# Experts' gathered rows turned by DMA transposes of their 16-bit halves in place of TensorE transposes

## The chip, the cores and the metric

The kernel runs on one core of a Trainium2 chip. The metric is the device time of one execution in microseconds; a single launch does everything, and the host only lays the inputs out.

## What is computed

The reference is a gated feed-forward layer with adapters (LoRA), followed by a mixture of eight experts, each token going to its best two. The second part is the one that the change touches:

```python
x = x + ffn(cond(x, ...), W_gate, b_gate, W_e, b_e)     # x: 2048 tokens of 1024

def ffn(y, W_gate, b_gate, W_e, b_e):                   # y: 2048 x 1024, W_e: 8 x 1024 x 1024
    logits = y @ W_gate + b_gate
    _, top_idx = jax.lax.top_k(logits, 2)
    y_all = relu(einsum('bsd,edh->bseh', y, W_e) + b_e)
    return take_along_axis(y_all, top_idx[..., None], axis=2).mean(axis=2)
```

All of it is float32. TensorE gets each float32 operand as a rounded high part and a low part (what rounding left), and each product is three matmuls: high by high, high by low, low by high.

## The kernel before, in words

Two groups of 1024 tokens go through the gated layer and leave y in DRAM (`y_scratch`). Then a table of rows is built: the 4096 pairs of token and expert are sorted by expert and padded to blocks of 128 rows, each block for one expert. There are 41 block numbers at most (`NB`); how many are used is known only at run time, and blocks from 32 on stand under a branch (`when`). In the profiled run 37 are used, numbers 0 to 36.

Five engines work on the blocks, each through its own list in order:

- **GpSimd (POOL)**, for b = 1, 2, ...: `y_lo(b+1)`, the low part of block b+1 (L837); `gather_y(b+3)`, which fetches 128 rows of y into `ybuf`, a ring of three buffers (L829); `add_bias(b)` (L847); `scatter(b)`, which adds the finished rows into the output by DMA (L855).
- **TensorE (PE)**: `one(b)` waits for both parts of block b (`s_tc`, `s_tlo`) and for the expert's weights (`s_el`), does 24 of its 48 matmuls, then `turn(b+1)`, eight 128 x 128 transposes of the next block's rows into PSUM (L2013), then the other 24. The last matmul raises `s_blk`. The rows must be turned because TensorE contracts over partitions, and a gathered row lies along one partition.
- **ScalarE (ACT)**, for b = 2, 3, ...: `blk_hi(b)` copies the turned block from PSUM to `ytp` (L1446) and, rounded, to `ring` (L1447); `blk_out(b-1)` waits for the end of block b-1's matmuls, copies their sums out of PSUM (L1457, raising `s_zc`), waits for the bias and applies relu (L1459).
- **VectorE (DVE)** rounds the next expert's weights (L1672) and takes their low parts (L1673).
- **SyncE (SP)** loads weights in eight pieces of 512 KB for each expert (L416, three buffers) and each expert's bias (L563).

`ytp` is one buffer: `blk_hi(b)` waits for `s_tlo`, so that POOL is done with block b-1 there, and for `s_blk`, so that `ring`'s half is free.

## Time and profile before

| | us |
|---|---|
| median of 3 runs | 1865.73 (1862.27 to 1865.85) |
| the profiled execution | 1862.27 |
| its span, first to last instruction | 1860.4 |
| PE busy in the span | 1817.3 (98%) |
| POOL busy | 1077.1 (58%) |
| ACT busy | 742.2 (40%) |
| mean granted TensorE clock, share of full | 0.991 |

The span is what the profile covers; 1.9 us of the execution lie outside it. Times in the views are counted from the span's start. Busy time of PE overstates its work, since its matmuls overlap: one is shown as 0.39 us, and the next starts 0.23 us after it. The blocks of experts fill the stretch from about 1400 us to the end.

### The profile page before, as it was taken

The numbers are of one execution on the slowest core, as the hardware profiler recorded it, in microseconds if no ns is written. First come the engines' busy times: TensorE is split into PE (matmuls) and PEld (weight loads), VectorE is DVE, ScalarE is ACT, GpSimd is POOL, SyncE is SP. The second block draws the span as 40 slices with busy tenths as digits, with TensorE's granted clock in tenths as the row PEclk, the third lists the DMA queues.
The fourth block names the chain that finished last, engine by engine and source line by source line (L and its number), as shares of the span: only waits on it lengthen the run. The fifth ranks groups of instructions, "written<-read, shape, count | busy, mean of one in ns | idle before, by whom it ended". The sixth has DMA issues, their size and how long they took to land. (4 is left out here: it accounts for less than half of the span.)

```text
span 1860.4 us, 24949 instructions
## 1 busy us (share of the span) xinstructions
PE 1817.3 (98%) x8583; PEld 1511.6 (81%) x8583; DVE 1252.9 (67%) x1500; ACT 742.2 (40%) x1054; POOL 1077.1 (58%) x643
## 2 busy tenths in 40 slices
PE   7899999999999999999999999999999999999997
PEld 6788888888888888888888887888877888888885
DVE  8878787885567797888888886477878543234400
ACT  5544444444543335444434444443322333333332
POOL 2678888873444454456656544444425666666664
PEclk9999999999999999999999999999998999999998
DMA  5556655645577655555665645676634775577543
GB/s 209 171 201 220 227 203 204 237 157 164 191 247 245 221 181 176 180 177 176 205 217 184 213 162 188 217 251 233 206 132 154 222 192 143 141 193 193 149 101 47
DMA packets 128395, 350.32 MB, mean 188 GB/s; under 512 B 15232, under 2 KB 17152, under 8 KB 128000
## 3 DMA queue, kind: packets, MB, share of 16 engines
q1 hardware_dynamic: 110320, 286.94, 45.3%
q0 software_dynamic: 17952, 61.75, 13.8%
q8 instruction: 77, 1.26, 0.3%
q14 instruction: 46, 0.38, 0.1%
HBM read 267.49 MB, written 90.05 MB: 192 GB/s over the span
## 5 line engine op out<-in xcount | busy, mean ns | idle before, releaser
L1680 PE MATMUL PS<-R,ring 128*128 128x512 f32 (+1 forms) x1800 | 709.0, 394 | 21.4 <-DVE R L939 9.3
L1681 PE MATMUL PS<-R,ring 128*128 128x512 f32 (+1 forms) x1800 | 703.7, 391 | 0.0
L1682 PE MATMUL PS<-R,ring 128*128 128x512 f32 (+1 forms) x1800 | 703.2, 391 | 0.0
L1680 PEld LDWEIGHTS PS<-R,ring 128*128 128x128 f32 x1800 | 339.9, 189 | 92.3 <-issue 14.9
L1682 PEld LDWEIGHTS PS<-R,ring 128*128 128x128 f32 x1800 | 339.2, 188 | 72.0
L1681 PEld LDWEIGHTS PS<-R,ring 128*128 128x128 f32 x1800 | 340.2, 189 | 66.0
L769 POOL TENSOR_TENSOR ring<-raw,ring 128x1024 fp32r<-128x1024 f32 x78 | 193.1, 2475 | 269.1 <-ACT ring L895 269.0
L1680 PE MATMUL PS<-ring,R 128*128 128x512 f32 x592 | 231.6, 391 | 1.7 <-DVE FT L1236 1.7
L1681 PE MATMUL PS<-ring,R 128*128 128x512 f32 x592 | 230.8, 390 | 0.0
L1682 PE MATMUL PS<-ring,R 128*128 128x512 f32 x592 | 230.4, 389 | 0.0
L748 POOL DMA_INDIRECT brw<-in_bgu,idx_b x88 | 95.3, 1083 | 227.8 <-DVE R L1060 188.9
L908 DVE TENSOR_TENSOR R<-FT,R 128x1024 fp32r<-128x1024 f32 x70 | 154.9, 2216 | 88.6 <-ACT R L904 88.3
L889 DVE TENSOR_TENSOR ring<-FT,ring 128x512 fp32r<-128x512 f32 x168 | 167.2, 1005 | 57.9 <-ACT ring L885 56.1
L1672 DVE CAST R<-raw 128x1024 fp32r<-128x1024 f32 x56 | 69.6, 1243 | 194.2 <-PE PS L1682 174.0
L885 ACT ACTIVATE ring<-FT 128x512 fp32r<-128x512 f32 x168 | 105.8, 631 | 214.6 <-PE PS L1682 122.0
L895 ACT ACTIVATE ring<-raw 128x1024 fp32r<-128x1024 f32 x78 | 82.7, 1060 | 245.6 <-PE PS L1682 164.8
L889 DVE TENSOR_TENSOR ring<-raw,ring 128x512 fp32r<-128x512 f32 x130 | 163.0, 1261 | 16.1 <-ACT ring L885 15.6
L885 ACT ACTIVATE ring<-raw 128x512 fp32r<-128x512 f32 x130 | 81.6, 630 | 193.6 <-PE PS L1682 147.8
L1142 DVE TENSOR_TENSOR FT<-FT,PS 128x512 f32<-128x512 f32 x168 | 110.6, 679 | 33.8 <-PE PS L1722 33.6
L1680 PEld LDWEIGHTS PS<-ring,R 128*128 128x128 f32 x592 | 111.1, 188 | 25.5 <-DVE FT L1236 2.5
L1682 PEld LDWEIGHTS PS<-ring,R 128*128 128x128 f32 x592 | 111.1, 188 | 23.6
L1681 PEld LDWEIGHTS PS<-ring,R 128*128 128x128 f32 x592 | 111.2, 188 | 21.6
(191 smaller groups left out, 2345.1 us busy)
## 6 DMA issues: line engine op xcount, KB each, us to landing
raw<-in_wp SPq DMA_DIRECT2D x124, 512.0 KB
act_scratch<-FT SPq DMA_DIRECT2D x140, 256.0 KB, 5.0
FT<-act_scratch SPq DMA_DIRECT2D x70, 512.0 KB, 4.3
raw<-in_we SPq DMA_DIRECT2D x64, 512.0 KB
ytp<-in_wgb SPq DMA_DIRECT2D x96, 256.0 KB
raw<-wt_scratch SPq DMA_DIRECT2D x40, 512.0 KB
out<-in_xn SPq DMA_DIRECT2D x17, 512.0 KB, 5.4
y_scratch<-FT SPq DMA_DIRECT2D x7, 1024.0 KB, 6.2
```

Of the source, the lines that this page charges most:

```text
L748: e.indirect_dma_start(out=brw[0:96, j * 512:(j + 1) * 512], out_offset=None, in_=bgu.rearrange("(r a) n -> r (a n)", a=2), in_offset=ioa( ...
L769: e.tensor_tensor(slot2(n, 1), pair(raw_t(i)), slot2(n, 0), ALU.subtract).then_inc(s_lp, 1)
L885: e.activation(slot(op(g, n), 0), w_src(g, n), ACT.Copy).then_inc(s_hi, 1)
L889: e.tensor_tensor(slot(op(g, n), 1), w_src(g, n), slot(op(g, n), 0), ALU.subtract).then_inc(s_lo, 1)
L895: e.activation(slot2(n, 0), pair(raw_t(i)), ACT.Copy).then_inc(s_hi, 2)
L908: e.tensor_tensor(a_ring(j, 1), raw_a(j), a_ring(j, 0), ALU.subtract).then_inc(s_al, 1)
L1142: e.tensor_tensor(c_tile(q, k), tile(E_T + [0, 2, 0, 1][k]), PS[:, bk + [1, 2, 3, 0][k], :], ALU.add).then_inc(s_c, 1)
L1672: link(e.tensor_copy(s_w_t(ex, k, 0), raw_t(i)))
L1680: e.matmul(out_, hi, whi, start=start, stop=False, skip_group_check=True)
L1681: e.matmul(out_, hi, wlo, start=False, stop=False, skip_group_check=True)
L1682: return e.matmul(out_, lo, whi, start=False, stop=stop, skip_group_check=True)
```

## The change

From block 4 on (`TB = 4`), TensorE no longer turns the gathered rows. ScalarE splits each gathered block into the upper and the lower 16 bits of its float32 values (`upper_lower`, two copies into `brw`, which is free by then), starts one DMA transpose of the 128 x 2048 values of 16 bits from its own queue (`across`, into tiles 15 and 16 of `FT`), and later weaves both halves back into float32 values in `ytp` (`blk_hi16`, two copies) before the rounded copy to `ring`. Blocks 0 to 3 keep the old way. `blk_out` is cut in two, `blk_z` (sums out of PSUM) and `blk_out` (relu), and `across` stands between them. `gather_y` waits for `upper_lower` instead of the TensorE transposes before it writes a buffer again.

```diff
         def gather_y(e, b):
-            if b >= 5:
+            if b in (5, 6):
                 e.wait_ge(s_tp, b - 2)
+            if b >= 7:
+                e.wait_ge(s_de, b - 6)
...
+        rows16 = brw[:, :].bitcast(U16)
+        cols16 = tile(SET_E, 2).bitcast(U16).rearrange("p (c r) -> p c r", r=128)
...
+        def halves(ap):
+            return ap.bitcast(U16).rearrange("p (n h) -> p h n", h=2)
+
+        def upper_lower(e, b):
+            e.wait_ge(s_gd[b % 3], 16 * ((b - 2) // 3 + 1))
+            h = halves(ybuf[:, b % 3, :])
+            e.activation(rows16[:, 0:1024], h[:, 1, :], ACT.Copy)
+            e.activation(rows16[:, 1024:2048], h[:, 0, :], ACT.Copy).then_inc(s_de, 1)
+
+        def across(e, b):
+            e.wait_ge(s_de, b - TB + 1)
+            if b > TB:
+                e.wait_ge(s_rc, b - TB)
+            e.dma_start_transpose(out=cols16, in_=rows16).then_inc(s_dt, 16)
+
+        def blk_hi16(e, b):
+            e.wait_ge(s_dt, 16 * (b - TB + 1))
+            e.wait_ge(s_tlo, b)
+            h = halves(ytp[:, :])
+            e.activation(h[:, 1, :], cols16[:, 0:8, :].rearrange("p k r -> p (k r)"), ACT.Copy)
+            e.activation(h[:, 0, :], cols16[:, 8:16, :].rearrange("p k r -> p (k r)"), ACT.Copy).then_inc(s_rc, 1)
+            e.wait_ge(s_blk, b)
+            e.wait_ge(s_rc, b - TB + 1)
+            e.activation(ring_t(b % 2, 0), ytp[:, :], ACT.Copy).then_inc(s_tc, 1)
...
             for b in range(2, NB):
-                when(e, used, b, blk_hi, e, b)
-                if b:
-                    when(e, used, b - 1, blk_out, e, b - 1)
+                when(e, used, b, blk_hi if b < TB else blk_hi16, e, b)
+                if b + 1 >= TB:
+                    when(e, used, b + 1, upper_lower, e, b + 1)
+                when(e, used, b - 1, blk_z, e, b - 1)
+                if b + 1 >= TB:
+                    when(e, used, b + 1, across, e, b + 1)
+                when(e, used, b - 1, blk_out, e, b - 1)
...
                 products(range(mid))
-                if b < 31:
+                if b + 1 < TB:
                     turn(b + 1)
...
             for b in range(2, NB):
-                if b >= 31:
-                    when(e, used, b + 1, turn, b + 1)
                 when(e, used, b, one, b)
```

ScalarE's list in the blocks of experts, before (two turns of the loop; FT here is the staging buffer of the results, PS is PSUM):

```order
780 L1446 ACTIVATE ytp<-PS 128x1024 [waits s_tlo,s_blk,s_tp]
781 L1447 ACTIVATE ring<-PS 128x1024
782 L1457 ACTIVATE FT<-PS 128x1024 [waits s_sc,s_blk]
783 L1459 ACTIVATE FT<-FT 128x1024 [waits s_ba]
784 L1446 ACTIVATE ytp<-PS 128x1024 [waits s_tlo,s_blk,s_tp]
785 L1447 ACTIVATE ring<-PS 128x1024
```

The same place in the changed kernel, one turn of the loop (its line numbers are its own; brw is the buffer of halves, and FT in rows 967 and 970 is `cols16` and `ybuf`):

```order
967 L1478 ACTIVATE ytp<-FT 128x1024 [waits s_tlo,s_dt]
968 L1479 ACTIVATE ytp<-FT 128x1024
969 L1482 ACTIVATE ring<-ytp 128x1024 [waits s_rc,s_blk]
970 L1464 ACTIVATE brw<-FT 128x1024 [waits s_gd2]
971 L1465 ACTIVATE brw<-FT 128x1024
972 L1491 ACTIVATE FT<-PS 128x1024 [waits s_sc,s_blk]
973 L1472 DMA_TRANSPOSE FT<-brw 128x16x128 [waits s_rc,s_de]
974 L1496 ACTIVATE FT<-FT 128x1024 [waits s_ba]
```

Four ScalarE instructions for each block have become seven and a DMA issue, and what the first of them waits for is no longer PE's `s_tp` but the DMA's `s_dt`.

TensorE's list in the middle of block 3, before (ident is the identity matrix, FT is `ybuf`):

```order
6237 L1681 MATMUL PS<-R,ring 128x512
6238 L1682 MATMUL PS<-R,ring 128x512
6239 L2013 MATMUL PS<-ident,FT 128x128 [waits s_tc,s_gd1]
6240 L2013 MATMUL PS<-ident,FT 128x128 x7
6241 L1680 ISA
6242 L1680 MATMUL PS<-R,ring 128x512
```

and in the changed kernel:

```order
6237 L1724 MATMUL PS<-R,ring 128x512
6238 L1725 MATMUL PS<-R,ring 128x512
6239 L1723 ISA
6240 L1723 MATMUL PS<-R,ring 128x512
6241 L1724 ISA
```

The eight transposes are gone there and in every later block, and nothing has taken their place on TensorE.

## Rows read from the trace of the kernel before

**Rows 1.** The page's chain that ended last: shares of the span by engine, by line.

```profile
PE 45%; DVE 1%; issue 1%; DMA 1%; ACT 0%; POOL 0%; POOLq 0%; SPq 0%; ACTq 0%; DVEq 0%
```

**Rows 2.** Busy time by 40 us stretch, granted clock (PEclk), DMA share, GB/s.

```profile
1560.00:1600.00 40.00, 40.00 (x190) 33.35 (x189) 21.95 (x16) 13.26 (x14) 26.92 (x14) 1.00 0.79 211
1600.00:1640.00 40.00, 40.00 (x191) 33.34 (x190) 13.87 (x10) 13.89 (x14) 25.97 (x14) 1.00 0.57 149
```

**Rows 3.** The copy of sums out of PSUM: duration min/median/max in ns, first and last start.

```profile
L1457 ACT ACTIVATE FT<-PS x37: 1024/1029/1030, 1415.8 to 1846.9; 128x1024 f32<-128x1024 f32 x37
```

**Rows 4.** ScalarE in time: start, us, line, operation [idle before <-releaser].

```profile
1470.21 1.03 ACT L1457 ACTIVATE FT<-PS 128x1024 f32<-128x1024 f32 x1 [3.51 <-PE PS L1682]
...
1600.05 1.03 ACT L1457 ACTIVATE FT<-PS 128x1024 f32<-128x1024 f32 x1 [3.54 <-PE PS L1682]
1603.71 1.06 ACT L1459 ACTIVATE FT<-FT 128x1024 f32<-128x1024 f32 x1 [2.62 <-POOL FT L847]
1606.37 1.03 ACT L1446 ACTIVATE ytp<-PS 128x1024 f32<-128x1024 f32 x1 [1.60 <-PE PS L2013]
1607.29 1.02 ACT L1447 ACTIVATE ring<-PS 128x1024 fp32r<-128x1024 f32 x1
1611.83 1.03 ACT L1457 ACTIVATE FT<-PS 128x1024 f32<-128x1024 f32 x1 [3.51 <-PE PS L1682]
...
1835.98 1.03 ACT L1457 ACTIVATE FT<-PS 128x1024 f32<-128x1024 f32 x1 [5.26 <-PE PS L1682]
...
1846.86 1.02 ACT L1457 ACTIVATE FT<-PS 128x1024 f32<-128x1024 f32 x1 [6.17 <-DMA out<-FT,sidx]
```

**Rows 5.** TensorE around one block's transposes, in time.

```profile
1616.61 0.39 PE L1681 MATMUL PS<-R,ring 128*128 x1
1616.84 0.40 PE L1682 MATMUL PS<-R,ring 128*128 x1
1617.07 1.04 PE L2013 MATMUL PS<-ident,FT 128*128 128x128 f32 x8
1617.87 0.47 PE L1680 MATMUL PS<-R,ring 128*128 x1
1618.18 0.39 PE L1681 MATMUL PS<-R,ring 128*128 x1
```

**Rows 6.** GpSimd in time, one block.

```profile
1601.28 2.39 POOL L847 TENSOR_TENSOR FT<-FT 128x1024 f32<-128x1024 f32 x1 [1.15 <-ACT FT L1457]
1605.05 1.59 POOL L855 DMA_INDIRECT out<-FT,sidx  x1 [1.37 <-ACT FT L1459]
1608.40 2.39 POOL L837 TENSOR_TENSOR ring<-ytp,ring 128x1024 fp32r<-128x1024 f32 x1 [1.76 <-ACT ring L1447]
1610.94 0.99 POOL L829 DMA_INDIRECT FT<-y_scratch,gidx  x1 [0.16 <-issue]
```

**Rows 7.** DMAs of the whole run: out<-in, count, KB each, median us from issue to landing.

```profile
FT<-in_be SPq DMA_DIRECT2D x8, 512.0 KB, 4.2
X<-in_xp SPq DMA_DIRECT2D x2, 512.0 KB, 11.6
FT<-y_scratch,gidx POOLq DMA_INDIRECT x36, 8.1
```

**Rows 8.** DMA from 1470 to 1846 us: packets, MB, share of 16 engines; then issues.

```profile
q0 software_dynamic: 8993, 32.78, 42.1%
q1 hardware_dynamic: 6912, 25.17, 19.2%
...
raw<-in_we SPq DMA_DIRECT2D x42, 512.0 KB
FT<-in_be SPq DMA_DIRECT2D x5, 512.0 KB, 4.1
out<-FT,sidx POOLq DMA_INDIRECT x32
FT<-y_scratch,gidx POOLq DMA_INDIRECT x30
```

**Rows 9.** SyncE's queue in time: issue of one expert's eight pieces of weights.

```profile
1510.20 20.74 SPq L416 DMA_DIRECT2D raw<-in_we  x8
```

**Rows 10.** TensorE's idle times early in the run, and the granted clock around them.

```profile
34.44 0.50 PE L1680 MATMUL PS<-R,ring 128*128 128x512 f32 x1 [1.88 <-DVE ring L889]
...
49.71 0.50 PE L1680 MATMUL PS<-R,ring 128*128 128x512 f32 x1 [3.82 <-DVE ring L889]
...
33.00:37.00 4.00, 2.56 (x11) 2.14 (x12) 3.88 (x7) 2.38 (x5) 2.46 (x3) 1.00 0.28 69
50.00:53.00 3.00, 3.00 (x9) 2.35 (x9) 2.94 (x6) 2.59 (x5) 0.00 (x0) 0.54 0.92 283
```

More of the change, by code:

```diff
@@ L10 @@
 U32 = mybir.dt.uint32
+U16 = mybir.dt.uint16
 ALU = mybir.AluOpType
@@ L23 @@
 NB = 41
+TB = 4
 RW = 3
@@ L273, in build @@
         s_blk, s_zr, s_sc = sem("s_blk"), sem("s_zr"), sem("s_sc")
+        s_de, s_dt, s_rc = sem("s_de"), sem("s_dt"), sem("s_rc")
         y_d = nc.dram_tensor("y_scratch", (T, H), F32).ap()
@@ L1447, in blk_hi, with blk_z @@
             e.activation(ring_t(b % 2, 0), tp, ACT.Copy).then_inc(s_tc, 1)
-        def blk_out(e, b):
+        def halves(ap):
[19 more added lines that the diff above has]
+            e.activation(ring_t(b % 2, 0), ytp[:, :], ACT.Copy).then_inc(s_tc, 1)
+        def blk_z(e, b):
             e.wait_ge(s_blk, b + 2)
@@ L1455, in blk_out @@
             z = PS[:, 4 + 2 * (b % 2):6 + 2 * (b % 2), :]
+            e.activation(sbuf2[:, 2 * (b % 2):2 * (b % 2) + 2, :], z, ACT.Copy).then_inc(s_zc, 1)
+        def blk_out(e, b):
             y = sbuf2[:, 2 * (b % 2):2 * (b % 2) + 2, :]
-            e.activation(y, z, ACT.Copy).then_inc(s_zc, 1)
             e.wait_ge(s_ba, b + 2)
@@ L1497, in _ @@
             blk_hi(e, 1)
+            blk_z(e, 0)
             blk_out(e, 0)
@@ L1500, in _ @@
             for b in range(2, NB):
-                when(e, used, b, blk_hi, e, b)
-                if b:
-                    when(e, used, b - 1, blk_out, e, b - 1)
+                when(e, used, b, blk_hi if b < TB else blk_hi16, e, b)
[5 more added lines that the diff above has]
+                when(e, used, b - 1, blk_out, e, b - 1)
+            when(e, used, NB - 1, blk_z, e, NB - 1)
             when(e, used, NB - 1, blk_out, e, NB - 1)
```

## The prediction

> **What bounds the kernel now.** I read the chain of waits first. It is TensorE almost alone, and every other engine has 1% or less [rows 1], so only what shortens or stalls TensorE moves the time. In the blocks of experts TensorE shows no gap at full clock (40.00 us busy of 40.00, PEclk 1.00), while ScalarE works 13 to 14 us and GpSimd 26 to 27 of each 40 [rows 2]. The change reaches only this stage.
>
> The beat of the stage stands in ScalarE's copies out of PSUM, each released by the last matmul of a block: 37 of them [rows 3], from 1600.05 to the next at 1611.83, so 11.78 us for a block; over 32 blocks, (1846.86 - 1470.21) / 32 = 11.77 [rows 4]. What a block takes without transposes also stands in the trace. The last block turns no successor, and it took 1846.86 - 1835.98 = 10.88 us [rows 4]. TensorE's own rows agree: between two matmuls there are 0.23 us, but 1.03 us (1616.84 to 1617.87) across the eight transposes and 0.31 after them [rows 5], so 0.80 + 0.08 = 0.88 us for the turn. I take 11.77 - 10.88 = 0.89 us.
>
> **What is removed.** The turns of blocks 4 to 36 go, 33 of them, which is 33 x 0.89 = 29.4 us if nothing else comes late. Nothing of that is hidden now, since TensorE has no gap.
>
> **What is added, and where it lies.** ScalarE has for each block two copies for the halves, two for the weaving where one copy to ytp stood, and the issue of a DMA. Its nearest row is the relu, SBUF to SBUF, 1.06 us for 1024 columns, where the next copy follows 0.92 us after a copy's start [rows 4]. Copies of 16-bit values with a stride are in no row. I cost them like the float32 copies: half that would be the most a narrower type could give, twice that the most a stride could take. So ScalarE goes from 4.1 to about 7.2 us of a block of 10.9. As busy time that is free; the order of the waits is what costs.
>
> Follow one block. Let 0 be the end of block b-1's matmuls, as ScalarE sees it. Copying the sums starts then. The transpose of block b+1 is queued behind that copy, so it is issued at about 1.0 (0.1 if the queue doesn't wait for the copy). It lands L later. Then come the two weaving copies (0.95 + 1.06), the wait for their own semaphore (0.05, my estimate) and the rounded copy (1.06), together 3.1 us; then GpSimd's low part, 0.09 us later and 2.39 long [rows 4, 6]; then TensorE may begin block b+1, with about 0.1 us for the semaphore. That is 1.0 + L + 3.1 + 0.1 + 2.4 + 0.1 = L + 6.7, and TensorE wants it at 10.9. As block b+1 then runs some 11.1 us with its first weight load and its last matmul's tail, two blocks take at least 17.8 + L. **First loop: one block takes (17.8 + L) / 2.** Behind the weaving on ScalarE stand the halves of block b+2 (two copies, 2.0), and only then the next copy of sums and the next transpose. **Second loop: one block takes L + 3.1 + 2.0 + 1.0 = L + 6.1.** The block takes the largest of 10.88 and these two. The point at which it is as long as before is L = 5.7 (second loop; 5.7 to 5.8 by the first). The bias and relu stay beside it: 1.03 + 2.39 + 1.06 us after the sums, so done at about 4.8, before the transpose has landed. GpSimd's gather is now issued after a later low part, about when block b ends, and has two blocks of time before its rows are wanted. Neither is on the path.
>
> **What L is** is the whole question, and the trace has no DMA transpose. Its nearest rows move the same 512 KB. From below: the bias loads, on a queue of the same kind and in this very stage, land after 4.2 us [rows 7]. From above: loads of x with others in front of them take 11.6 us, and the gathers of this stage, which start on GpSimd, 8.1 [rows 7]. What the transpose meets in the DMA engines can be read too. In 376 us the gathers and scatters hold 42.1% for 62 transfers, 2.6 us of all 16 engines each, and the loads 19.2% for 47, 1.5 us each [rows 8]. The gather is issued at about the end of a block, as the transpose is, and its data would run beside it. I take half of that overlap: L = 4.2 + 1.3 = 5.5. Where weights are being loaded, a piece of 1.5 us stands in the way as well: L = 7.0. One expert's loads are issued over 20.7 us [rows 9], and six experts have theirs in this stretch (five bias loads in it, one just before), so 6 x 20.7 / 11.8 = 10.5 of the 33 blocks.
>
> The sum: 22.5 blocks with L = 5.5 take 11.65 us, a gain of 0.12 each, -2.7 us. 10.5 blocks with L = 7.0 take 13.1 us (second loop), +1.33 each, +14.0 us. Together +11 us on 1862.3 us of the profiled execution, 1873.6. The median is 3.5 us above that execution, so the forecast for a median is 1877.
>
> **Rule against row.** The row nearest to a plain transfer gives L = 4.2. The Trainium skill says in "Advanced Engine Details and Errata", section "X-Bar Transpose (TRN2)", that such transposes are as fast as regular DMAs, about 90% of a plain copy; by this rule L would stay near that row, and the result is rival B. The Trainium skill also says, in "VectorE: DVE Perf Modes", section "The three transpose paths", that a 128 x 128 transpose of 16-bit values takes 1309 ns by DMA and 390 ns on TensorE. This transpose has 16 such tiles, so if they went one after another at that figure, it would be an estimate of 21 us, which speaks against the change and is rival D. No run here shows either.
>
> **The rivals.**
>
> *A, the forecast:* L between 5 and 7, a gain in quiet blocks and a larger loss where weights are loaded. For it: DMA engines are 0.57 to 0.79 busy before the transpose adds its share [rows 2]. Own range 1862 to 1905. Chance 0.30.
>
> *B, hidden:* L stays at 4.2 or below. The first loop gives 11.0, so -0.77 x 33 = -25 us, and at L under 3.9 the full 29.4: 1836 to 1841. For it: the bias loads' 4.2 us were measured in the same stage. Against: those were issued with no gather at the same moment. Chance 0.22.
>
> *E, issue ahead:* the DMA leaves 0.1 us after the block's end, beside the copy of sums. Both loops lose 0.9 us. L = 5.5 gives 11.2 (-0.57 x 22.5 = -13 us), L = 7.0 gives 12.2 (+0.43 x 10.5 = +4.5), together -8: 1857. Chance 0.20.
>
> *C, as slow as a gather:* L = 8.1 in every block. Second loop 14.2, +2.43 x 33 = +80 us: 1946. TensorE then idles 3.3 us in each block. The clock stayed at 1.00, which is 2.4 GHz, after an idle time of 1.88 us, and fell to about half, 1.2 GHz, after one of 3.82 [rows 10]; if it fell here, each block could lose 1.6 us more (eight matmuls of 0.43 instead of 0.23 us). It decides from L = 5.8 on. Against: the gather's 8.1 us hold GpSimd's own making of descriptors. Chance 0.18.
>
> *D, tiles in a row:* the transpose passes its 16 column groups slowly, L = 11.6 or more. Second loop 17.7, +5.9 x 33 = +196 us: 2060 and up. Chance 0.10.
>
> That the change doesn't do what it says I can rule out: the list of TensorE has no transpose after block 2's. In blocks 32 to 36 every step stands under its own branch, ten more for ScalarE in a turn; before, these blocks kept the beat of 11.8 us, but ScalarE had slack then. I allow 0 to 3 us in all.
>
> **How the numbers follow.** The likeliest case is A. A measurement of this kernel can tell about 0.2%, 3.7 us. Faster (under 1862): B 0.22, most of E 0.13, a little of A 0.02, so 0.37. Within: the rest of E 0.06 and 0.06 of A, 0.12. Slower: the rest of A, C and D, 0.51. The range takes in B whole, E, A and C without its clock term: 1837 to 1950, which leaves out D and the worst of C, 0.15 or so, and the hair below B.
>
> **What would show it.** The transpose's time to landing, of which the copies out of PSUM give the beat: with L = 4.2 a beat of 11.0, with 5.5 of 11.65, with 7 of 13.1. ScalarE's weaving copy should wait for the DMA in each block. If TensorE's wait in front of a block's first matmul is for GpSimd's low part and about as long as the beat less 10.9, the loops are right; if it is for weights, the DMA engines are the limit, which I have not costed. Blocks under way of weight loads should be longer than others; if all are alike, my splitting of L is wrong. The forecast falls if the transposes need twice a plain transfer's time, or if 16-bit copies on ScalarE take 2 us.

## The result and the profile after

The changed kernel takes 1954.55 us, the median of 4 runs (1944.23 to 1979.04), against 1865.79 (1862.27 to 1870.13, 4 runs) for the kernel before on the same chip: a ratio of 1.0456, 95% interval 1.0407 to 1.0505. Ratios, here and below, leave out runs over 1.5% above the fastest of their kernel (here 1979.04), while medians are of all runs, so the loss is 89 us by the medians and 85 by the ratio. The forecast was 1877 with a range to 1950; the sign came out as the likelier one, the size is past the end of the range. The profiled execution took 1944.23 us, span 1942.4, which is 82.0 us more than the 1860.4 of before.

The page: busy time, and the chain that ended last, which answers to [rows 1].

```profile
PE 1818.2 (94%) x8319; PEld 1501.4 (77%) x8319; DVE 1247.3 (64%) x1500; ACT 858.5 (44%) x1153; POOL 1078.1 (56%) x643
...
PE 37%; DMA 7%; issue 3%; ACT 3%; DVE 1%; POOL 0%; POOLq 0%; ACTq 0%; SPq 0%; DVEq 0%
```

TensorE had 98% of the span before and 94% now, and 7% of the chain is a DMA. The list of waits says which one (1480 to 1920 us; engine and line, who released it, us in total, times, longest):

```profile
POOL ring L844 <- ACT ring L1482: 125.8, 31, 15.1
...
PE PS L1723 <- issue: 77.0, 20, 14.6
ACT ytp L1478 <- DMA FT<-brw: 71.0, 24, 13.8
DVE R L1715 <- DMA raw<-in_we: 70.5, 21, 11.3
```

Read it from the last but one line upwards: the weave (L1478) waits for the transpose, the low part on GpSimd (L844) waits for ScalarE, and a block's first matmul (L1723) waits, 20 times, for the low part. ("Issue" names no engine here; the rows below show that GpSimd ends 0.2 us before.) VectorE's wait for weights is not on this path: it rounds weights blocks ahead.

The transposes themselves (L1472; duration of the issue in ns, min/median/max):

```profile
L1472 ACTq DMA_TRANSPOSE FT<-brw x33: 1333/1873/6562, 1448.8 to 1904.6; - x33
...
DMA to landing us min/median/max: 4.3/6.3/18.6
```

One turn of ScalarE's loop in time (start, us), beside [rows 4]:

```profile
1610.02 1.00 ACT L1491 ACTIVATE FT<-PS 128x1024 f32<-128x1024 f32 x1
1610.15 3.69 ACTq L1472 DMA_TRANSPOSE FT<-brw  x1
1615.36 1.06 ACT L1496 ACTIVATE FT<-FT 128x1024 f32<-128x1024 f32 x1 [4.33 <-POOL FT L854]
1619.24 1.38 ACT L1478 ACTIVATE ytp<-FT 128x1024 uint16<-128x1024 uint16 x1 [2.82 <-DMA FT<-brw]
1620.47 1.36 ACT L1479 ACTIVATE ytp<-FT 128x1024 uint16<-128x1024 uint16 x1
1621.92 1.06 ACT L1482 ACTIVATE ring<-ytp 128x1024 fp32r<-128x1024 f32 x1
1622.89 1.04 ACT L1464 ACTIVATE brw<-FT 128x1024 uint16<-128x1024 uint16 x1
...
1624.78 1.00 ACT L1491 ACTIVATE FT<-PS 128x1024 f32<-128x1024 f32 x1
```

This is the second loop of the prediction, closed: the issue comes 0.13 us after the copy of sums starts, the weave 9.09 us after the issue, and the next copy of sums 5.54 us after the weave, without a wait of its own. 0.13 + 9.09 + 5.54 = 14.76 us for this block, where [rows 3, 4] had 11.78.

A transpose with nothing beside it, the last one:

```profile
1904.60 1.33 ACTq L1472 DMA_TRANSPOSE FT<-brw  x1
1908.07 1.06 ACT L1496 ACTIVATE FT<-FT 128x1024 f32<-128x1024 f32 x1 [2.59 <-POOL FT L854]
1909.03 1.35 ACT L1478 ACTIVATE ytp<-FT 128x1024 uint16<-128x1024 uint16 x1
```

Its first packet starts 1.2 us after the issue, its last ends at 3.8, it lands at 4.3, and the weave has no wait for it. One with a gather issued 0.1 us ahead of it, while no weights were loaded:

```profile
1509.59 0.99 POOL L836 DMA_INDIRECT FT<-y_scratch,gidx  x1 [0.16 <-issue]
1509.68 1.33 ACTq L1472 DMA_TRANSPOSE FT<-brw  x1
...
1520.02 1.35 ACT L1478 ACTIVATE ytp<-FT 128x1024 uint16<-128x1024 uint16 x1 [5.69 <-DMA FT<-brw]
```

And the worst one, on ScalarE, on GpSimd, on SyncE and on TensorE:

```profile
1675.46 1.45 ACTq L1472 DMA_TRANSPOSE FT<-brw  x1
...
1694.05 1.35 ACT L1478 ACTIVATE ytp<-FT 128x1024 uint16<-128x1024 uint16 x1 [13.82 <-DMA FT<-brw]
```

```profile
1673.95 0.99 POOL L836 DMA_INDIRECT FT<-y_scratch,gidx  x1
...
1680.76 1.98 POOL L862 DMA_INDIRECT out<-FT,sidx  x1 [1.62 <-ACT FT L1496]
1697.82 2.79 POOL L844 TENSOR_TENSOR ring<-ytp,ring 128x1024 fp32r<-128x1024 f32 x1 [15.07 <-ACT ring L1482]
```

```profile
1666.76 35.28 SPq L421 DMA_DIRECT2D raw<-in_we  x8
```

```profile
1685.85 0.39 PE L1725 MATMUL PS<-R,ring 128*128 x1
1700.85 0.79 PE L1723 MATMUL PS<-R,ring 128*128 x1 [14.61 <-issue]
```

Weights were being loaded, a gather was issued 1.5 us ahead of the transpose and a scatter 5.3 us behind it. What the DMA engines did meanwhile (busy time of PE, PEld, DVE, ACT, POOL; granted clock; DMA share; GB/s; a share can pass 1, since packets' times overlap):

```profile
1675.00:1680.00 5.00, 5.00 (x24) 4.14 (x23) 2.77 (x4) 1.86 (x2) 2.51 (x1) 1.00 1.15 280
1680.00:1685.00 5.00, 5.00 (x24) 4.14 (x23) 2.91 (x3) 0.23 (x1) 1.98 (x1) 1.00 1.24 89
1685.00:1690.00 5.00, 1.24 (x6) 0.70 (x4) 0.00 (x0) 0.00 (x0) 0.00 (x0) 1.00 1.38 92
1690.00:1695.00 5.00, 0.00 (x0) 0.00 (x0) 0.31 (x1) 0.95 (x1) 0.00 (x0) 0.61 0.83 159
```

This is not a queue of useful work: the engines show full and move a third of what they moved just before. By the packet records, one packet of 256 bytes took 81 ns on average in this transpose and 21 ns in the lone one.

**Where the 82 us are.** From the copy of sums of block 2 to that of block 35 lie 33 blocks, each with a transpose issued at its start. Nine of them, those where the weave started over 8.6 us after the issue, took 158.8 us, 52.9 more than 9 x 11.77. The other 24 took 12.95 us on average, 28.3 more than before. Together 81. The nine cost more than their own length: TensorE begins the next block late, so the nine blocks right behind them took 13.9 us on average, the other 15 took 12.4. TensorE's ledger, by the starts of its matmuls from 1440 us on, says the same in other terms: no gap before, 20 gaps now, 91.5 us long, which are 87.0 over the normal spacing of 0.227 us; seven of them (15.0, 12.6, 8.9, 7.3, 6.8, 6.3 and 5.7 us) make 62.6. Matmuls that start 0.40 to 0.60 us after the one before, most of them 0.43, as where the granted clock is at its lower level, 1.2 GHz, were 1 and are 89, which is 19.1 us more. Less the 29.4 of the turns: +77 of the 82.

The DMA engines from 1470 to 1940 us, beside [rows 8]:

```profile
q0 software_dynamic: 9359, 34.08, 35.7%
q10 hardware_dynamic: 64532, 16.27, 24.8%
q1 hardware_dynamic: 7344, 26.74, 18.5%
```

A transpose is 2080 packets, 2048 of 256 bytes and 32 of 4, and it holds the 16 engines for 2.8 us when alone and for 0.248 x 470 / 31 = 3.8 us on average.

### The profile page after: what moved, and what is told of

Same layout as the page of the kernel before. It is cut to its first block, busy times and chain, and to the rows that moved or that the text cites. A ratio compares the mean times of both kernels' runs of the same rounds, so it can differ in the third digit from the quotient of the medians.

```text
span 1942.4 us, 24603 instructions
## 1 busy us (share of the span) xinstructions
PE 1818.2 (94%) x8319; PEld 1501.4 (77%) x8319; DVE 1247.3 (64%) x1500; ACT 858.5 (44%) x1153; POOL 1078.1 (56%) x643
## 3 DMA queue, kind: packets, MB, share of 16 engines
q1 hardware_dynamic: 110320, 286.94, 43.9%
## 4 chain that ended last, share of the span: by engine, by line
PE 37%; DMA 7%; issue 3%; ACT 3%; DVE 1%; POOL 0%; POOLq 0%; ACTq 0%; SPq 0%; DVEq 0%
PE PS L1723 11%; PE PS L1724 11%; PE PS L1725 11%; DMA FT<-brw 7%; PE PS L1838 1%; ACT ytp L1478 1%; ACT ytp L1479 1%; ACT ring L1482 1%; PE PS L1979 1%; PE PS L1765 1%; DMA FT<-act_scratch 0%; DMA out<-FT,sidx 0%; PE PS L1972 0%; DVE FT L1298 0%; PE PS L2056 0%
## 5 line engine op out<-in xcount | busy, mean ns | idle before, releaser
L1723 PE MATMUL PS<-R,ring 128*128 128x512 f32 (+1 forms) x1800 | 717.5, 399 | 101.9 <-issue 87.7
L1724 PE MATMUL PS<-R,ring 128*128 128x512 f32 (+1 forms) x1800 | 711.9, 395 | 0.0
L1725 PE MATMUL PS<-R,ring 128*128 128x512 f32 (+1 forms) x1800 | 710.5, 395 | 0.0
L1723 PEld LDWEIGHTS PS<-R,ring 128*128 128x128 f32 x1800 | 345.1, 192 | 184.6 <-issue 109.4
L1725 PEld LDWEIGHTS PS<-R,ring 128*128 128x128 f32 x1800 | 344.1, 191 | 73.6
L1724 PEld LDWEIGHTS PS<-R,ring 128*128 128x128 f32 x1800 | 345.3, 192 | 68.1
L1715 DVE CAST R<-raw 128x1024 fp32r<-128x1024 f32 x56 | 62.1, 1108 | 269.3 <-PE PS L1725 194.8
L1723 PE MATMUL PS<-ring,R 128*128 128x512 f32 x592 | 231.6, 391 | 1.7 <-DVE FT L1243 1.7
L896 DVE TENSOR_TENSOR ring<-FT,ring 128x512 fp32r<-128x512 f32 x168 | 174.3, 1048 | 56.2 <-ACT ring L892 54.7
L896 DVE TENSOR_TENSOR ring<-raw,ring 128x512 fp32r<-128x512 f32 x130 | 158.3, 1226 | 16.2 <-ACT ring L892 15.8
L844 POOL TENSOR_TENSOR ring<-ytp,ring 128x1024 fp32r<-128x1024 f32 x36 | 89.9, 2499 | 139.5 <-ACT ring L1482 136.6
L1723 PEld LDWEIGHTS PS<-ring,R 128*128 128x128 f32 x592 | 111.1, 188 | 25.4 <-DVE FT L1243 2.5
L1725 PEld LDWEIGHTS PS<-ring,R 128*128 128x128 f32 x592 | 111.1, 188 | 23.6
```

Of the source, the lines that this page charges most:

```text
L844: e.tensor_tensor(ring_t(b % 2, 1), ytp[:, :], ring_t(b % 2, 0), ALU.subtract).then_inc(s_tlo, 1)
L896: e.tensor_tensor(slot(op(g, n), 1), w_src(g, n), slot(op(g, n), 0), ALU.subtract).then_inc(s_lo, 1)
L1715: link(e.tensor_copy(s_w_t(ex, k, 0), raw_t(i)))
L1723: e.matmul(out_, hi, whi, start=start, stop=False, skip_group_check=True)
L1724: e.matmul(out_, hi, wlo, start=False, stop=False, skip_group_check=True)
L1725: return e.matmul(out_, lo, whi, start=False, stop=stop, skip_group_check=True)
```

## The experiments

All times are medians, and ratios are against the kernel before in the same session, with 95% intervals. The experiments e1 to e6 and e8 to e15 start from the changed kernel, e7 and e16 to e18 from the kernel before.

**e1: the gather out of the transpose's way.**

```diff
-                when(e, used, b + 3, gather_y, e, b + 3)
                 when(e, used, b, add_bias, e, b)
+                when(e, used, b + 3, gather_y, e, b + 3)
```

> The changed kernel with one pair of lines swapped on GpSimd: the gather of block b+3 is issued behind the bias of block b, not in front of it, so some 2.4 us later against the transpose. Theory (collision): a transpose is long when the gather's packets meet it; in the changed kernel it lands in 4.3 us when the gather starts 0.65 us or more later and no weights are loading, and in 5.5 to 10.7 when they start together. So here the median from issue to landing falls from 6.3 to 4.3 to 4.6 us, quiet blocks take about 10.9 to 11.1 us, and the whole takes 20 to 50 us less than the changed kernel. Rival (the chain of ScalarE is long by itself, the transpose is 6.3 us long because of its size): the median stays at 6.3 and the time within 5 us of the changed kernel.

1901.17 us, 1.0199 (1.0173 to 1.0225): 53 us of the 89 are gone by moving one line of GpSimd's list, which starts the gather some 3 us later in the block. Transposes' last packets, 5.8 us after the issue in the changed kernel, now end 4.0 us after the issue in the median; five take over 8, all while weights are loaded.

**e2: the weights small.** Experts 2 to 7 load 64 of 1024 columns of each piece (the rest of the weights is left out).

```diff
-            else:
+            elif a < 2:
                 src = we[a, b]
+            else:
+                e.dma_start(raw_t(i)[:, 0:64], we[a, b][:, 0:64]).then_inc(s_raw[i % RW], 16)
+                return
```

> The changed kernel, but of the weights of experts 2 to 7 only the first 64 of 1024 columns of each piece are loaded, so the blocks of these experts compute with old weights; every wait and every instruction stays. Theory (collision): the transposes of 9.1 to 18.6 us, nearly all within a burst of weight loads, vanish; two near 10.5 us that met only a gather may stay. The median of landing falls to about 5.7 us, the longest to 11, and the whole takes 30 to 50 us less than the changed kernel. Rival (only the gather matters): the long ones stay and the time is within 10 us of the changed kernel.

1890.79 us, 1.0168 (1.0139 to 1.0198). Last packets at 5.4 us in the median, 8.3 at most, and 64 us less than the changed kernel, somewhat more than was expected. So both neighbours cost, and each about alike: e1 leaves the bursts (the stretches in which an expert's weights are loaded), e2 leaves the gather.

**e5: both at once.** The two edits together.

> Both cures at once: the gather behind the bias, and of the weights of experts 2 to 7 only 64 of 1024 columns loaded (so these experts compute with old weights). Theory (a transpose is long only where other packets meet it; what is left then is the gain of 0.89 us a block that was forecast for a hidden transpose): every transpose's last packet ends 3.9 to 5.2 us after the issue, nearly every block takes 10.9 us, and the time is 1835 to 1845 us, 20 to 28 under the kernel before. Rival (a part of the loss is in the new ScalarE chain whatever the transpose takes): blocks stay at 11.5 us or more and the time stays at or over 1860.

1862.26 us (10 runs), 0.9982 (0.9962 to 1.0002). Every transpose's last packet ends within 5.3 us of the issue, and all that the change lost has come back, 92 us. The gains of e1 and e2 add up to 117, so they overlap. (The kernel before was not run with the small weights; TensorE had no gap there for them to close.) But the gain that rival B promised for such a landing has not. Transposes and beat then stood like this:

```profile
1648.75 1.02 ACT L1494 ACTIVATE FT<-PS 128x1024 f32<-128x1024 f32 x1 [0.88 <-PE PS L1728]
1648.81 1.92 ACTq L1475 DMA_TRANSPOSE FT<-brw  x1
1652.39 1.06 ACT L1499 ACTIVATE FT<-FT 128x1024 f32<-128x1024 f32 x1 [2.62 <-POOL FT L857]
1653.36 1.35 ACT L1481 ACTIVATE ytp<-FT 128x1024 uint16<-128x1024 uint16 x1
```

The weave no longer waits for the DMA but stands behind the relu, which stands behind the bias. The 33 blocks take 11.73 us each, 10 of them under 10.95.

**e3: the transpose ahead of the copy of sums on ScalarE.**

```diff
-                when(e, used, b - 1, blk_z, e, b - 1)
                 if b + 1 >= TB:
                     when(e, used, b + 1, across, e, b + 1)
+                when(e, used, b - 1, blk_z, e, b - 1)
```

> The changed kernel with the transpose of block b+1 issued before the copy of block b-1's sums out of PSUM, so that it no longer waits for the end of block b-1. Theory (two loops): ScalarE's loop loses the copy of 0.94 us and the first loop's tie to the end of a block goes; at a landing of 6.3 us a block takes 11.0 instead of 12.0. Blocks with long landings gain 1 us each at most, so the whole gains 15 to 30 us. Rival (the long landings alone make the time, and an earlier issue meets the gather and scatter differently): under 10 us either way.

1992.98 us, 1.0617 (1.0543 to 1.0691): slower than the changed kernel by 38 us, or 30 by the ratios, where a gain was expected. The median landing fell, from 6.3 to 5.9 us; the loss is in seven transposes, all issued while weights were loaded, that landed after 20 to 30.3 us. An issue that is earlier is no gain if its company is worse.

**e4 and e6: transposes two blocks ahead.** Two buffers each for the halves and for the turned tiles; in e6 the gather stands behind the bias as well.

```diff
-        rows16 = brw[:, :].bitcast(U16)
+        rows16 = [brw[:, :].bitcast(U16), brw2[:, :].bitcast(U16)]
...
-                if b + 1 >= TB:
-                    when(e, used, b + 1, across, e, b + 1)
+                if b + 2 >= TB:
+                    when(e, used, b + 2, across, e, b + 2)
```

> The changed kernel with two buffers of halves and two of turned rows: the transpose is issued two blocks ahead of its use, and the gather four. Theory (latency on the path): a landing of up to about 14 us is hidden, so all but one to three blocks take 10.9 us, TensorE's waits fall from 91 us to under 20, and the time is 1840 to 1855 us, below the kernel before. Rival (the DMA engines or ScalarE's seven instructions are the limit, not the latency): a block stays at 12 us or more, and the time stays above 1890 us.

> The kernel with transposes two blocks ahead, with the gather of block b+4 behind the bias. All weights are loaded. Theory (collision): the two-ahead kernel was spoilt because more transfers met, with the last packet at 6.5 us in the median and 30 at most; the later gather brings the median to about 4.2 and, since up to 14 us are now hidden, only weight bursts of over that cost anything: 1845 to 1870 us. Rival (the DMA engines are near their limit with gather, scatter, transpose and weights): the long ones stay and the time is 1890 us or more.

e4: 1927.05 us, 1.0317 (1.0264 to 1.0371). e6: 1900.94, 1.0199 (1.0167 to 1.0231), no better than e1 with one block of lead. A block of lead gives a landing 10.9 us more, which would hide all but the worst ones if waiting for them were the only cost. Both forecasts were missed. In e4 14 of 33 transposes took over 8 us to their last packet, up to 30.5, and ScalarE waited 50.5 us for gathers (1480 to 1920 us), for which it had not waited before: gathers too now landed late. That the extra transfers in flight slowed one another is the likely reading.

**e7: unused transposes in the kernel before.** For the blocks 3 to 31 a transpose of 512 KB that nobody reads, behind the copy of sums; ScalarE waits for each one's landing before it issues the next.

```diff
             e.activation(y, z, ACT.Copy).then_inc(s_zc, 1)
+            if b > 3:
+                e.wait_ge(s_dt, 16 * (min(b, 32) - 3))
+            if 3 <= b < 32:
+                e.dma_start_transpose(out=cols16, in_=rows16).then_inc(s_dt, 16)
```

> The kernel before, TensorE transposes and all, to which ScalarE adds one DMA transpose per block (from block 3 to 31) behind its copy of sums; nobody uses the result, and ScalarE only waits a block later that the last one has landed. Theory (latency on the path, not traffic by itself): the transposes are as long as in the changed kernel where they meet gathers and weights, yet the time stays within 10 us of the kernel before, because TensorE waits for none of them. Rival (the traffic itself starves gathers or weights): 1890 us or more.

1894.15 us, 1.0184 (1.0134 to 1.0235): 29 us without any data depending on a transpose, where under 10 was expected. The place in ScalarE's list:

```profile
1480.47 1.03 ACT L1462 ACTIVATE FT<-PS 128x1024 f32<-128x1024 f32 x1 [2.81 <-PE PS L1691]
1483.63 5.57 ACTq L1466 DMA_TRANSPOSE FT<-brw  x1
1489.24 1.06 ACT L1468 ACTIVATE FT<-FT 128x1024 f32<-128x1024 f32 x1 [7.74 <-issue]
```

The issue waits 2.1 us behind the copy of sums for the landing before, and then is itself under way for 5.57 us, while the relu stands ready behind it.

**e17 and e18: the same transfers from SyncE.** Unused transposes again, one for each of the blocks 4 to 31, issued by SyncE between and behind the loads of weights; in e18 a plain copy of the same 512 KB, from and to the same tiles, stands in the transpose's place.

```diff
+        def dummy(e, b):
+            e.wait_ge(s_zc, b + 1)
+            if b > 4:
+                e.wait_ge(s_dt, 16 * (b - 4))
+            e.dma_start_transpose(out=cols16, in_=rows16).then_inc(s_dt, 16)
```

```diff
-            e.dma_start_transpose(out=cols16, in_=rows16).then_inc(s_dt, 16)
+            e.dma_start(out=cols16, in_=rows16).then_inc(s_dt, 16)
```

> The kernel before with 28 unused DMA transposes of 512 KB, one for each of the blocks 4 to 31, issued by SyncE when the block's sums are copied; nothing but SyncE waits for them. Theory (ScalarE's queue, held by the issue, made e7's 28 us): ScalarE is free here, the gathers and scatters have slack, so within 8 us of the kernel before, 1858 to 1873 us. Rival (the traffic: gathers, scatters and weights land late whoever issues the transposes): slower by 15 us or more, 1880 to 1900 us, with TensorE waiting for GpSimd or VectorE.

> As e17, but each of the 28 transfers is a plain copy of the same 512 KB from one tile to the other, without a transpose. If the bytes are what costs, it is as e17; if the transpose's 2080 small packets are, it is at 1860 to 1870 us even where e17 is slower. The copy should hold the 16 DMA engines for some 1.5 us in place of 2.8 and land in 4 to 5 us.

e17: 1869.16 us (10 runs), 1.0028 (1.0012 to 1.0044). e18: 1863.27 (10 runs), 0.9999 (0.9986 to 1.0012). The issue and the landings, of e17 and then of e18:

```profile
L575 SPq DMA_TRANSPOSE FT<-brw x28: 1317/3584/6921, 1472.1 to 1804.9; - x28
...
DMA to landing us min/median/max: 4.2/7.4/17.8
```

```profile
L575 SPq DMA_DIRECT2D FT<-brw x28: 465/471/522, 1476.0 to 1794.4; - x28
...
DMA to landing us min/median/max: 3.0/4.8/8.2
```

The transposes of e17 hold their queue as long as those of e7 (3.6 us in the median beside 3.8) and land no earlier than those of the changed kernel (7.4 beside 6.3), yet cost 5 us. So the slowness of a transpose costs little as traffic; it costs where ScalarE stands behind it. And the bytes are not what makes it slow: the copy moves the same 512 KB in 144 packets (queue 1 had 110320 in the kernel before and 114352 with the 28 copies) where the transpose has 2080, is issued in 0.47 us whatever else runs, and costs nothing that can be measured.

**e8: half a transpose.** From block 5 on only the upper halves are turned (the lower halves keep what stood there).

```diff
-            e.dma_start_transpose(out=cols16, in_=rows16).then_inc(s_dt, 16)
+            if b == TB:
+                e.dma_start_transpose(out=cols16, in_=rows16).then_inc(s_dt, 16)
+            else:
+                e.dma_start_transpose(out=cols16[:, 0:8, :], in_=rows16[:, 0:1024]).then_inc(s_dt, 16)
```

> The changed kernel with half of the transpose: from block 5 on only the 1024 upper halves are turned, and the lower halves woven in are those of block 4. An undisturbed transpose has its first packet 1.3 us after the issue and its last at 3.9, so half of it should end at 2.6 us; with collisions the median falls from 5.9 to about 4 us. By the loops a block gains 0.65 to 1.3 us: 1900 to 1925 us. Rival (the wait is for other transfers in front, not for the transpose's own packets): the median falls by less than 0.8 us and the time by less than 15 us.

1913.15 us, 1.0255 (1.0227 to 1.0283): 41 us less than the whole transpose, nearly half of the 89 that the change lost, and within the forecast. Last packets end 4.2 us after the issue in the median, up to 13.1 among the half ones. The loss goes with the size of the transpose. And so does the hold of the queue by the issue, which is nearly gone (32 half transposes, ns, min/median/max; the whole ones of the changed kernel had 1333/1873/6562):

```profile
L1475 ACTq DMA_TRANSPOSE FT<-brw x32: 1247/1249/1343, 1478.4 to 1875.8; - x32
```

Two halves, one behind the other, were not tried.

**e10: TensorE's turns back in.** The changed kernel with eight transposes of the identity in blocks 4 to 35, whose result nobody reads.

```diff
+                elif 4 <= b < 36:
+                    for k in range(8):
+                        e.transpose(PS[:, 2 * (b % 2) + k // 4, (k % 4) * 128:(k % 4 + 1) * 128], ident[:, :], ident[:, :])
```

> The changed kernel with TensorE's eight transposes put back into blocks 4 to 35, on the identity matrix, with no wait of their own and a result that nobody reads. It tells what their removal was worth in the changed kernel. Theory (a block's pace is set by two loops through ScalarE; one holds TensorE's block for every second block, the other not at all): 5 to 18 us more than the changed kernel, of the 29.4 that the same work costs in the kernel before. Rival (the removed time is paid in full, the loss is a separate sum): 29 us more.

1981.91 us (1958.9 to 2011.31), 1.0573 (1.05 to 1.0646), 27 us over the changed kernel by the medians, 22 by the ratios, where 29.4 is the full price. The two kernels' runs spread over 35 and 52 us, and the ratios' intervals leave anything from about 5 to 38 us, so this decides neither for the theory (5 to 18) nor for the rival (29).

**e9: two ahead, late gather, small weights.** e6 and the edit of e2 together.

> Two blocks ahead, the gather behind the bias, and of the weights of experts 2 to 7 only 64 of 1024 columns loaded (so these experts compute with old weights). Theory (with one block of lead the first loop has no slack even at a landing of 4.3 us, so every hiccup of the kernel with the late gather and small weights was paid): with two blocks of lead and nothing long in the DMA engines, blocks take 10.9 to 11.0 us and the time is 1836 to 1846 us. Rival (ScalarE's seven copies, the weaving at 1.37 us each, or the wait for the gather hold a block at 11.5 us): 1855 us or more.

1864.97 us (10 runs), 0.9996 (0.998 to 1.0012). Last packets at 3.9 us in the median and 5.9 at most, with a block of lead to spare, and still 11.52 us a block. The rival was right. ScalarE and GpSimd in such a block, which show what is left:

```profile
1609.50 1.03 ACT L1496 ACTIVATE FT<-PS 128x1024 f32<-128x1024 f32 x1 [1.05 <-PE PS L1731]
1609.56 1.82 ACTq L1477 DMA_TRANSPOSE FT<-brw  x1
1613.14 1.06 ACT L1501 ACTIVATE FT<-FT 128x1024 f32<-128x1024 f32 x1 [2.62 <-POOL FT L859]
1614.11 1.35 ACT L1483 ACTIVATE ytp<-FT 128x1024 uint16<-128x1024 uint16 x1
```

```profile
1610.72 2.39 POOL L859 TENSOR_TENSOR FT<-FT 128x1024 f32<-128x1024 f32 x1 [1.80 <-ACT FT L1496]
...
1617.90 2.40 POOL L849 TENSOR_TENSOR ring<-ytp,ring 128x1024 fp32r<-128x1024 f32 x1 [1.75 <-ACT ring L1487]
```

Copy of sums, bias, relu, weave, rounded copy, low part: from 1609.50 to 1620.30, 10.8 us without a DMA in it, in a beat that should be 10.88, so that nothing in it may come late. This third chain is in no step of the prediction. The rival named the gather as well, and ScalarE did wait for it in front of the halves (waits from 1480 to 1850 us; in e5 the same wait made 10.7 us, 8 times):

```profile
ACT brw L1469 <- DMA FT<-y_scratch,gidx: 12.9, 11, 2.6
```

How the 0.64 us that a block takes over 10.88 divide between the two is not shown.

**e11 and e12: the whole work, weights one piece at a time.** e11 is e1 and e12 is e6, each with one piece of weights in flight from expert 2 on.

```diff
+                if a >= 2:
+                    e.wait_ge(s_raw[(i - 1) % RW], 16 * ((i - 1) // RW + 1))
```

> The gather behind the bias, all weights loaded, but each 512 KB piece of weights of experts 2 to 7 issued only when the piece before it has landed, so that one is in flight instead of up to three. Theory (a transpose in a burst is long by the number of pieces that it meets): transposes in bursts fall from 8 to 11 us to 5 to 8, and the time from 1901 to 1875 to 1890 us. Rival (one piece hurts as much as three, or the weights now come late): 1895 us or more, with TensorE waiting for weights in the second case.

> Two blocks ahead, late gather, one piece of weights in flight, all weights loaded: the version with most chance to beat the kernel before. Theory: bursts of up to 8 us are hidden by the lead, blocks take 11.0 us on the whole, 1850 to 1870 us. Rival (the second half of the burst, the gather's landing and the hold on ScalarE's queue still cost some microseconds in each of six bursts): 1880 us or more.

e11: 1881.13 us, 1.0108 (1.0082 to 1.0134). e12: 1876.67, 1.0077 (1.0058 to 1.0096), between its forecast and its rival's, the best of the versions that do the whole work, and slower than before.

**e13 to e15: the third chain taken apart.** On ScalarE the weave of block c+2 stands ahead of the relu of block c; the transpose of block c+3 stays behind the sums of block c, as in e6. GpSimd's order changes too: the low part comes a turn earlier, ahead of the gather and the scatter, and the gather one block earlier than in e6. e13 is with all weights, e14 with one piece in flight, e15 with small weights.

```diff
             for b in range(1, NB):
-                when(e, used, b + 1, y_lo, e, b + 1)
-                when(e, used, b + 3, gather_y, e, b + 3)
                 when(e, used, b, add_bias, e, b)
+                when(e, used, b + 2, y_lo, e, b + 2)
+                when(e, used, b + 5, gather_y, e, b + 5)
                 when(e, used, b, scatter, e, b)
...
+            for c in range(1, NB):
+                when(e, used, c, blk_z, e, c)
+                when(e, used, c + 3, across, e, c + 3)
+                when(e, used, c + 2, blk_hi if c + 2 < TB else blk_hi16, e, c + 2)
+                when(e, used, c, blk_out, e, c)
+                when(e, used, c + 4, upper_lower, e, c + 4)
```

> Transposes issued three blocks ahead of their ring copy, the weave of block b+2 ahead of the relu of block b on ScalarE, gather moved behind y_lo on POOL and a block earlier, weights as in the changed kernel. Theory (a third chain, sums copy, bias, relu, weave, ring copy, y_lo, of 10.8 us held the blocks of e9 and e12; with the weave ahead of the relu it is 9.4 us and has slack against a beat of 10.88): against e6, 1900.9 us, the quiet blocks come down to about 11 us and the lead hides transposes of up to some 12 us, so 1850 to 1885 us. Rival (the queue of ScalarE, held by the transposes while weights are in flight, as in e7, costs the 28 us whatever the lead): 1885 to 1910 us.

> As e13, with one weight piece in flight for the experts from the third on. Theory (third chain): e12's 1876.7 us less about 0.5 us for each of some 30 blocks and less the waits that the longer lead hides, so 1840 to 1860 us, faster than the kernel before by 0.3 to 1.4%. Rival (something else sets the 11.3 to 11.7 us: TensorE's clock or the traffic itself): 1862 to 1880 us, no faster than before.

> As e13, with experts 2 to 7 loading 64 of 1024 weight columns at a time (the rest of the weights is left out). Theory (third chain): the blocks run at 10.9 to 11.1 us instead of e9's 11.3 to 11.7, so 1836 to 1848 us. Rival (the blocks are bound by TensorE and its clock or by another wait): 1855 to 1866 us, as e5 and e9.

e13: 1930.13 us (1909.59 to 1965.25), 1.0352 (1.0305 to 1.0398). e14: 1917.73, 1.0207 (1.0142 to 1.0272). e15: 1859.76 (1847.68 to 1873.99, 10 runs), 0.9975 (0.9947 to 1.0002). All three missed; e15 came where its rival had put it. The third chain was real, but relieving it brought something as dear: 16 of e15's 33 blocks ran under 10.95 us where e9 had 9, and three over 14.5 where e9 had none. One of those three:

```profile
1588.78 1.03 ACT L1496 ACTIVATE FT<-PS 128x1024 f32<-128x1024 f32 x1 [1.31 <-PE PS L1731]
1588.84 5.60 ACTq L1477 DMA_TRANSPOSE FT<-brw  x1
1594.55 1.36 ACT L1483 ACTIVATE ytp<-FT 128x1024 uint16<-128x1024 uint16 x1 [4.74 <-issue]
...
1607.62 1.03 ACT L1496 ACTIVATE FT<-PS 128x1024 f32<-128x1024 f32 x1 [6.51 <-DMA out<-FT,sidx]
```

With the relu behind the weave, the scatter of the block before is issued at the same moment as the transpose (both at 1588.8), and the transpose's last packet came after 18.2 us where e9's never came after 5.9. Its own weave stands one turn of the loop later and did not wait; the issue, 5.60 us, held the weave behind it, and the scatter made the next copy of sums 6.5 us late. As the orders of ScalarE and of GpSimd were changed together, no run tells which of the two brought the scatter, the gather and the transpose together.

**e16: control.** The kernel before with one piece of weights in flight.

> The kernel before with one weight piece in flight for the experts from the third on, no DMA transposes. Theory: weight bursts cost the kernel before nothing, since its gathers and scatters wait for nothing of ScalarE, so 1860 to 1870 us. Rival (the bursts hold the kernel before too, and pacing them is a gain of its own): under 1855 us, and then e14 is to be held against this one.

1865.4 us (10 runs), 1.0003 (0.999 to 1.0016): pacing the weights is worth nothing by itself, so what it gave e11 and e12 it gave to the transposes.

## Why the prediction was wrong, step by step

- **What bounds the kernel:** right. Nothing but TensorE's gaps and its clock moved the time.
- **What is removed, 29.4 us:** right as far as it can be seen. The last block, which turns none, still takes 10.9 us, and quiet blocks of e1, e5 and e9 take 10.88. e10, with 5 to 38 us for the turns, is too wide to add to that.
- **When the transpose is issued:** rival E had it, 0.13 us after the copy of sums starts.
- **The loops:** right in form. The second loop, with that issue, was L + 5.2; measured it is 5.7 and the time from the issue to the weave. The 0.5 us are the weaving copies, 1.38 and 1.36 us where the relu's 1.06 was taken, less 0.2 in the copies behind them. The wait for their own semaphore, put at 0.05 without a row, measured 0.09. The first loop shows in pairs: the worst block and the one behind it took 24.13 + 14.33 = 38.5 us, where 17.8 + L is 36.4 and the lower clock gives 1.8 of the rest.
- **L in quiet blocks, 5.5:** of about the right size as a mean (the 24 ordinary blocks landed after 5.8 us on average and had the weave at 6.2, which takes in the wait behind the relu), wrong in its make-up. Alone a transpose lands in 4.3 us, as the bias loads of [rows 7] do. The Trainium skill says in "Advanced Engine Details and Errata", section "X-Bar Transpose (TRN2)", that such transposes are as fast as regular DMAs: a lone one agrees with the load (4.3 beside 4.2 us), but not with the nearer comparison, e18's copy between the same tiles, whose shortest took 3.0; and in company it does not hold at all (e17's 7.4 us in the median and 17.8 at most, beside e18's 4.8 and 8.2). The Trainium skill's 1309 ns for one tile by DMA ("VectorE: DVE Perf Modes", section "The three transpose paths") does not add up over tiles, as rival D took it to: 16 tiles landed in 4.3 us, not in the estimated 21.
- **L beside a gather, + 1.3 for half an overlap:** the first step that failed. Where the gather was issued 0.1 us ahead of the transpose and no weights were loaded (1509.68 and 1888.24 us), L was 10.3 and 10.7, so + 6; in two others, with the gather within 0.1 us (1648.97 and 1785.42), it was 7.2 and 7.8, so + 3. With the gather 0.65 us or more behind and no weights, L was 4.3 to 7.2. e1 priced it over the run: 53 us.
- **L in a burst of weights, 7.0:** the second, and the larger by size in one block. I added the time of one piece in the way, 1.5 us, as if transfers took turns. In the two worst ones (1675.46 and 1748.68) the transpose's packets took 81 and 58 ns instead of 21, L went to 18.6 and 17.1. L was over 8 in nine blocks; six of them stood in bursts, a seventh 2 us behind one. Both steps priced sharing by adding busy times from [rows 8]; the runs show that a transpose in company loses far more than the neighbour's time. e5, which takes both neighbours out of the way, gives back 92 us. This is the cause of the miss.
- **The issue priced at nothing:** the third. It holds ScalarE's queue for 1.33 us at least and 6.56 at most. In the changed kernel each hold was over before the landing, so there it is not seen to add anything; it does where something stands behind it that needn't wait for the landing (e15's 5.60 us). e7 against e17 shows what standing behind transposes costs ScalarE, their issue and their landing taken together: 29 us against 5. The two are not separated.
- **The clock:** I charged it to rival C alone. After the long gaps the granted clock fell (0.61 in 1690 to 1695 us), and 88 more matmuls at the wider spacing cost 19.1 us, of which 17.2 fall into the 24 ordinary blocks. These took 12.95 us, where the second loop gives 11.9 with 6.2 us from issue to weave: 25 us in all, of which the clock explains up to 17. The rest goes with the late start of TensorE behind a long block, in the first loop.
- **"The bias and relu stay beside it":** right for most of the changed kernel (in six blocks the weave began 0.8 to 2.0 us after the landing, behind the relu), wrong for the forecasts of rivals B and E. With L at 4.3 the chain by way of bias and relu, 10.8 us, has no slack (e9), and e5 shows that B's 1836 to 1841 was not there to be had by a faster landing alone.
- **What the prediction named as its test:** that blocks under loads of weights would be longer came true, and so did TensorE's wait for the low part; that the DMA engines might be the limit, it said, was not costed.
- **The rivals:** C had the nearest time, 1946, for a wrong reason: not all blocks at 8.1 us, but nine at 12.1 on average and 24 at 5.8, with the clock term on top. That number was near by luck.

**What stays open.** Why a transpose in company is slowed so much, and why its issue is held, no run shows; that it is bound to the many small packets fits e8 and e18, which also differ in other ways (e8 in bytes, e18 in the kind of transfer). How much of e7's 29 us is the hold alone wasn't tried. Nor was the changed kernel with its transposes issued by SyncE: e17's transposes fed nobody, so that such a move would help where TensorE waits for the landing is not shown. No version beat the kernel before: e5, e9 and e15 equal it, each with most of the weights left out, and e12 is 0.77% slower with the whole work.

## What to carry to other kernels

Price a DMA that takes over an engine's work by its latency in the company that it will have, not by its lone landing plus its neighbours' busy time, and give the range the worst company. Ask on whose queue it is issued and what stands behind it there: transposes that nobody needed cost 29 us from ScalarE, which is on the path and also waited for their landings, and 5 us from SyncE, which is not. And when one chain of waits is relieved, look for the next of equal length before promising the whole gain.

## What the hardware showed that I had not expected

- A DMA transpose of 512 KB from SBUF to SBUF is 2080 packets. Alone it lands in 4.3 us; beside gathers, scatters and loads of weights in up to 18.6 us in the changed kernel and 30 in e3. In the worst of the changed kernel the DMA engines show full and move 89 GB/s. A plain copy of the same bytes in the same places took 8.2 us at most.
- The issue of a transpose takes 1.32 us at least, even with a gather beside it (1.33 at 1509.68), and up to 6.9 with one transpose in flight (14.5 in e4 and 14.7 in e13, which run further ahead), on either queue; that of half a transpose 1.25 to 1.34; that of a plain copy 0.47 to 0.52 us.
- ScalarE's copies of 16-bit values differ by which side is strided: 1.04 us with the strided side read (L1464), 1.34 to 1.39 with it written (L1478).
